# Gather holds, the place of the turns, and the opening products of a DLRM tower kernel on one core

## The reference

```python
e = jnp.stack([tbl_0[ids[:, 0]], ..., tbl_25[ids[:, 25]]], axis=1)      # (512, 26, 128)
combined = jnp.concatenate((dense_features[:, None, :], e), axis=1)      # (512, 27, 128)
interactions = jnp.einsum('bfd,bgd->bfg', combined, combined)
z = jnp.concatenate((dense_features, interactions[:, iu, ju]), axis=1)   # iu, ju: upper triangle
h = jnp.concatenate([z, dense_features], axis=1)                         # (512, 607)
h = jnp.maximum(h @ W_top1 + b_top1, 0.0)                                # 607 x 512
h = jnp.maximum(h @ W_top2 + b_top2, 0.0)                                # 512 x 256
y = h @ W_top3                                                           # 256 x 1
```

## Time and profile before

| | |
|---|---|
| median of the runs | 125.9 us (124.06 to 126.88) |
| the profiled execution | 124.81 us, span 123.0 us |
| TensorE matmuls busy | 104.2 us, 85% |
| VectorE, ScalarE busy | 65.4 us, 48.1 us |
| GpSimd busy | 65.7 us, of it 65.0 us in 60 gathers |
| chain that ended last | TensorE 83%, "issue" 13%, VectorE 2%, ScalarE 1% |

### The profile page before, as it was taken

One profiled execution on the slowest core, in us unless ns is written; L12 is line 12 of the kernel. 1 busy time (PEld: TensorE's weight loads), 2 busy tenths in 40 slices (PEclk: granted clock), 3 DMA queues, 4 the chain that ended last, 5 costly groups with the idle time before them and its releaser, 6 DMA issues.

```text
span 123.0 us, 3436 instructions
## 1 busy us (share of the span) xinstructions
PE 104.2 (85%) x1516; PEld 87.9 (71%) x1516; DVE 65.4 (53%) x110; ACT 48.1 (39%) x81; POOL 65.7 (53%) x66
## 2 busy tenths in 40 slices
PE   6999999999999999962178996289995299998993
PEld 6787888888888888831067895177992278996991
DVE  2599999999899996820001742105540106451411
ACT  4542979197794931300000462002541102730321
POOL 3887888579878887877500887503778305000000
PEclk9999999999999999999555999756999558999999
DMA  3799999999211112121200111200112100000000
GB/s 57 236 400 365 402 398 408 410 392 368 80 43 45 45 43 48 44 63 43 64 5 5 43 43 43 64 0 0 45 43 64 43 0 20 23 0 0 0 0 1
DMA packets 3949, 13.51 MB, mean 110 GB/s; under 512 B 1315, under 2 KB 1317, under 8 KB 3302
## 3 DMA queue, kind: packets, MB, share of 16 engines
q1 hardware_dynamic: 2018, 9.48, 20.5%
q0 software_dynamic: 1920, 3.94, 11.2%
q10 hardware_dynamic: 4, 0.00, 0.0%
HBM read 13.42 MB, written 0.00 MB: 109 GB/s over the span
## 4 chain that ended last, share of the span: by engine, by line
PE 83%; issue 13%; DVE 2%; ACT 1%
PE bank L365 17%; PE prod L408 13%; PE bank L414 13%; PE prod L365 12%; PE bank L374 7%; PE bank L504 6%; PE prod L433 4%; PE bank L321 4%; PE bank L325 3%; PE bank L445 2%; DVE inter_s L585 1%; PE bank L438 1%; PE prod L421 1%; PE bank L421 0%; DVE xT L575 0%
## 5 line engine op out<-in xcount | busy, mean ns | idle before, releaser
L313 POOL DMA_INDIRECT emb<-in_tbl,ids_sb x60 | 65.0, 1083 | 38.3 <-PE prod L408 19.3
L522 DVE TENSOR_SCALAR mask<-ids_h,ids_sb 128x1024 fp32r<-128x1024 int16 (+1 forms) x48 | 31.5, 699 | 2.2 <-issue 0.8
L408 PE MATMUL prod<-xT 128*27 128x27 f32 x1024 | 16.8, 215 | 14.7 <-issue 14.2
L408 PEld LDWEIGHTS prod<-xT 128*27 128x27 f32 x1024 | 13.6, 128 | 18.8 <-issue 17.4
L585 DVE STREAM_TRANSPOSE inter_s<-prod 128x288 f32<-128x288 f32 (+1 forms) x8 | 4.6, 611 | 26.3 <-PE prod L408 26.3
L365 PE MATMUL bank<-mask,high 128*128 128x512 f32 x46 | 15.2, 393 | 0.0
L365 PE MATMUL bank<-mask,low 128*128 128x512 f32 x46 | 15.0, 390 | 0.0
L414 PE MATMUL bank<-pairs,w_sb 117*128 117x128 f32 x96 | 12.7, 282 | 0.1
L414 PEld LDWEIGHTS bank<-pairs,w_sb 117*128 117x128 f32 x96 | 11.6, 191 | 0.7 <-ACT pairs L696 0.5
L531 DVE TENSOR_TENSOR low<-table,high 128x1024 fp32r<-128x1024 f32 (+1 forms) x9 | 11.7, 1301 | 0.0
L374 PE MATMUL bank<-ident,emb 128*128 128x128 f32 x60 | 10.5, 310 | 0.9 <-issue 0.9
(11 more groups left out here) (55 smaller groups left out, 118.1 us busy)
## 6 DMA issues: line engine op xcount, KB each, us to landing
table<-in_resident SPq DMA_DIRECT2D x3, 1024.0 KB
w_sb<-in_weights SPq DMA_DIRECT2D x1, 1792.0 KB
table<-in_resident SPq DMA_DIRECT2D x1, 1280.0 KB
table<-in_resident SPq DMA_DIRECT2D x4, 256.0 KB
emb<-in_tbl,ids_sb POOLq DMA_INDIRECT x60
ids_h<-in_other_ids SPq DMA_DIRECT2D x1, 896.0 KB
table<-in_resident SPq DMA_DIRECT2D x1, 640.0 KB
ids_h<-in_pair_ids SPq DMA_DIRECT2D x1, 256.0 KB
```

Of the source, the lines that this page charges most:

```text
L313: nc.gpsimd.indirect_dma_start(out=rows(t, c), out_offset=None, in_=gathered[c], in_offset=bass.IndirectOffsetOnAxis(ap=ids_sb[:, i:i + 1] ...
L408: mm = nc.tensor.matmul(prod[SLOT_PITCH * q:SLOT_PITCH * q + SLOTS, i, 0:SLOTS], x, x, start=True, stop=True)
L522: nc.vector.tensor_scalar(made(step)[:, 0:n, :], ids_h[:, 2 * b:2 * b + n, :], col_sb[:, row:row + 1], None, ALU.is_equal).then_inc(s_mask, 1)
```

## The change

Four edits. `hold` is gone, so GpSimd waits only where a gather would overwrite rows not yet turned. In passes 2 and 3 nothing stands between the two halves of the products: group 0 of the next tile is turned behind them, with group 1; only the first pass turns group 0 of tile 1 between the halves, with the dense part. `turn_next` gets a branch for that. Ahead of the lookups the products of ones are 3 and then 2 of 128 columns (before: 4 and 7 of 64 columns), and then 6 that are 32 wide in rows and columns.

```diff
-WARM_UP, WARM_KEEP = 4, 7
-WARM_COLUMNS = 64
+WARM_UP, WARM_KEEP, WARM_NARROW = 3, 2, 6
+NARROW = 32
...
-            def hold(t, i):
-
-
-                if (t, i) == (1, 0):
-                    pool.wait_ge(s_used, first_step[2])
-                if (t, i) == (1, 8):
-                    pool.wait_ge(s_used, first_step[3] + 2)
-                if (t, i) == (2, 0):
-                    pool.wait_ge(s_used, first_step[4] + 3)
-                if (t, i) == (2, 6):
-                    pool.wait_ge(s_used, first_step[5] + 3)
-                if (t, i) == (2, 10):
-                    pool.wait_ge(s_prod, 1)
-                if (t, i) == (3, 0):
-                    pool.wait_ge(s_l1, 2)
-                if (t, i) == (3, 4):
-                    pool.wait_ge(s_prod, 2)
-                if (t, i) == (3, 9):
-                    pool.wait_ge(s_l1, 4)
-                if (t, i) == (3, 13):
-                    pool.wait_ge(s_prod, 3)
...
                     for c in range(first, first + n):
-                        hold(t, c)
                         i = t * GATHERED + c
...
+            def turn_second(some):
+                for g in some:
+                    pe.wait_ge(s_gather[1][g], 16 * GROUPS[g][1])
+                    turn(1, g)
...
                     with nc.tensor.If(p < TILES):
                         for g in some:
-                            bank_free(g)
-
-                            pe.wait_ge(s_gather[1][g], (p + 1) * (8 * GROUPS[g][1]))
-                            turn(1, g)
+                            if g:
+                                bank_free(g)
+
+                                pe.wait_ge(s_gather[1][g], (p + 1) * (8 * GROUPS[g][1]))
+                                turn(1, g)
+                            else:
+                                with nc.tensor.If(p > 1):
+                                    pe.wait_ge(s_gather[1][g], 32 * GROUPS[g][1])
+                                    turn(1, g)
...
-            def keep_busy(n):
+            def keep_busy(n, rows=P):
                 for _ in range(n):
-                    nc.tensor.matmul(half_bank[1][:, 0:WARM_COLUMNS], warm, warm[:, 0:WARM_COLUMNS], start=True, stop=True)
+                    nc.tensor.matmul(half_bank[1][0:rows, 0:rows], warm[:, 0:rows], warm[:, 0:rows], start=True, stop=True)
...
             keep_busy(WARM_KEEP)
+            keep_busy(WARM_NARROW, NARROW)
             look_up_first()
...
                 products(range(MATMULS // 2))
-                turn_next(p, (0,))
                 with nc.tensor.If(p < 2):
+
+                    turn_second((0,))
                     dense_part(slice(0, P), (0, 1))
                 products(range(MATMULS // 2, MATMULS)).then_inc(s_prod, 1)
...
-                turn_next(p, (1,))
+                turn_next(p, (0, 1))
```

## The result

The changed kernel takes 137.0 us (median of 4 runs, 135.42 to 141.1) against 125.87 us (4 runs, 124.06 to 126.88). The ratio is 1.085, with a 95% interval of 1.062 to 1.108. The forecast was 131.0 us, with a range up to 133.5 us: the direction was right, the size too small by about half.

What follows compares the result with a forecast made beforehand. Behind the lookups GpSimd, too, was taken to bound the kernel, its gathers slowing TensorE's products. Later passes 1 and 2, less 6.4 us in pass 3, gave span 129.0 against 123.0, so 130.8, put at 131.0 us; range 123.5 to 133.5.

Steps and rivals of the forecast that it cites:

- The mechanism in the loop: Products: while gathers are issued, TensorE gets 2 to 4 records per us after 17 to 39 fast ones.
- the forecast case: Pass 1: both halves of the products crawl beside gathers; 131.0 us, own range 128.5 to 133.5, chance 0.52.
- The rival that the second half escapes: Pass 1: gathers slow its second half too late, products end at 72.2; 127.2 to 127.4 us, chance 0.20.
- the crawl of its own length: Products: a gather only sets the crawl off, it ends by itself after 5 to 8 us; 119.1 us, chance 0.14.
- the gathers that are not the cause: Products: the crawl belongs to the first half whatever GpSimd does; 124.7 us, chance 0.14.
- Lookup holds: Lookups: GpSimd waited once, 1.00 us where 0.30 is usual; without it gathers come 0.7 us earlier, bounds nothing to 1.0.
- the loop's 6 us: Four passes of the loop: later products in passes 1 and 2, 6.4 us back in pass 3; span 6.0 us more.
- The opening: Ahead of the lookups: first lookup near 5.7 instead of 7.39, 0.9 us gained, worth nothing in the forecast.
- upper and lower six: First lookup's products: six upper take 2.67 us, end near 8.4; six lower end near 10.65, against 11.54.
- The turns: Passes 3 and 4: the four turnings moved between the products add 0.4 us each time.

Runs made afterwards that it cites:

- n_gather: Kernel before without the 30 gathers of tiles 2 and 3, computed from rows of tiles 0 and 1; slow chip: 103.95 us against 126.22.
- b_none3: Kernel before with all of hold() and its call removed, old turns and opening; slow chip: 132.82 us against 125.3, ratio 1.068.
- sp_loads2: Kernel before without the 30 gathers of tiles 2 and 3, SyncE's queue loading 24 blocks of rows instead; quick chip: 104.3 us against 106.95.
- a_all: Changed kernel with the nine holds put back (new opening and new turns alone); slow chip: 123.98 us against 125.56, ratio 0.986.
- after3: The changed kernel run a third time, on a slow chip: 132.39, 141.44 and 145.89 us against 125.56 for the kernel before.
- a_oldopen: Changed kernel with the old products of ones (4 and 7 of 64 columns); slow chip: 132.73 us against 125.56, ratio 1.057.
- b_warm: Kernel before with the new products of ones alone; quick chip: 105.98 us against 106.58, ratio 0.996.
- b_turns: Kernel before with the new place of the turns alone, holds and opening as before; slow chip: 123.33 us against 126.22.
- before_again: The kernel before, unchanged, run again for its trace on a quick chip: 106.84 us.

## Why the prediction was right or wrong

*The mechanism in the loop was right, on the slow chips: gathers beside the products make TensorE crawl.* `n_gather` shows the cause (22 us go with the gathers), `b_none3` the steps. The forecast for the changed kernel against what `b_none3` measured: first half of pass 1 ends at 68.3, measured 69.0; gather 45 at 69.7, 70.71; second half ends at 76.9, 77.2; gather 49 at 78.3, 79.03; pass 2 fast again at 93.3, 94.8; pass 3 starts at 104.8, 106.3; span 129.0, 130.5. `b_none3` still turns group 0 between the halves, so it is a neighbour of the forecast case, not the same. In the changed kernel itself the steps of pass 1 could be seen only in part, since its first half ran free. The rival that the second half escapes fell (50 fast records, then a crawl to 76.3); so did the crawl of its own length and the gathers that are not the cause. The Trainium skill (SBUF — State Buffer, "SBUF: two separate sides") has the rule that a DMA and a compute operation can't slow each other. Read as the prediction read it, that gathers can't be what slows the products, it doesn't hold here: 126.22 us with the 30 gathers, 103.95 without, and the measurement decides. For the transfer alone the trace of `sp_loads2` agrees with it, on a quick chip (1.27 us a half). Which path gathers and engines share was not found.

*The step that failed is the term "Lookup holds".* It read one wait of 1.00 us, took from it that the gathers come 0.7 us earlier, and had no price for the lookups themselves. The argument beside it was that layers and turns run under gathers without idle time, which holds for the lookups of the kernel before, too. But the crawl isn't tied to products: the traces show it in VectorE's and ScalarE's masks, and once each in two traces GpSimd itself is late. The changed kernel's trace has its first product 24.0 us later, and 7.7 us given back in the loop, since by then most gathers were through. That sum, not the loop's 6 us, makes the long executions. What starts this crawl, and whether taking the lookup holds away is what lets it run on, stays open: `a_all` suggests the second, no experiment shows it.

How the measured 11 us divide is only roughly known. Without the holds and with clean lookups the ratio is 1.068 (`b_none3`); the change as a whole has 1.085, and the intervals overlap. The rest is probably the lookups' crawl. By its own sum the forecast should also have been 131.9 and not 131.0: 129.0 + 1.8 is the profiled execution, and the runs' median lies 1.1 us above that. The executions in which the lookups are clean (`b_none3`, 132.35) or may be (132.39 in `after3`; 131.68, 132.51 and 132.95 in `a_oldopen`) come close to it. All four of the first comparison, 135.42 and up, don't.

*The opening came out near the forecast, in part by luck.* First lookup at 5.7, measured 5.86; upper and lower six done at 10.65, measured 10.74, against 11.53. But two terms in between were off and made up for each other: the upper six took 3.31 us and not 2.67, since they waited for masks, and the lower six 1.57 and not 2.25. The wide products of ones took 0.275 us each (6 in 1.65), not 0.23; with that price the 12 narrow ones took (1.93 - 4 x 0.275) / 12 = 0.07, where 0.08 was taken. In other traces with the new opening the lower six took 1.36 to 2.46 us, and in two of them nothing was gained by their end: 11.51 in `a_all`, 12.03 in `b_warm`. The opening's 0.4% on a quick chip (`b_warm`, 0.992 to 1.000) can hardly be told from nothing, and on a slow one it was not measured alone.

*The turns were undervalued.* I had them at plus 0.4 us twice. With one branch between the halves and not three, the 256 records of a free pass take 2.56 us, against 3.09 before (110.08 to 113.17); and `b_turns` gained some 2% on a slow chip.

*The condition of the chip was not thought of at all.* The kernel before is 19 us slower on a slow chip than on a quick one, and the crawls were what I took for a property of the kernel. On a quick chip the sign is the other: 0.991.

For a slow chip the holds stay. With them, the new turns alone (`b_turns`) and the new turns with the new opening (`a_all`, three executions, 0.986, 0.972 to 0.999) both came out 1 to 2% faster, and the runs don't say which is the better. On a quick chip neither was run.

## What to carry to other kernels

Idle time named "issue", on several engines at once and only while GpSimd's indirect DMAs run, may be a cost of the gathers: take the gathers out once and see what goes. A wait that idles its own engine for 1 us may be what lets others recover, so its price is not read from its own idle time. And where a kernel stands idle without a releaser, run it on a second chip before tuning the schedule around it: here one and the same change is 1% faster or 8% slower.

## What the runs showed of the hardware

- The same program takes 106.6 to 107.0 us on two chips and 125.3 to 126.2 us on three; without 30 gathers it takes 104 us on a slow one. The two levels of the clock, the 0.94 us of a gather and the matmuls' own rates are the same; the mean granted clock is not, 0.90 to 0.93 on the slow chips and 0.98 to 1.00 on the quick ones and in `n_gather`.
- In the crawl TensorE's product records come in groups of 1 to 6, 0.7 us or twice that apart (80.66 to 85.56 in the changed kernel: 46 fast, then 22 in 4.9 us). Even on a quick chip gathers stretch 128 records from 1.27 to 1.81 us, at the full clock. That the gathers slow the supply of instructions is a reading that fits engines without a missing input; no row shows it. The packets that load instructions are not what is slowed, as far as the page tells: the larger of their two queues has 4 packets in the kernel before on a slow chip, with 0.2% of the time of the 16 DMA engines, and 4 with 0.3% in `before_again` on a quick one, so about 4 us (0.002 x 16 x 123.0) and 5 us (0.003 x 16 x 104.7) for the four.
- Loads of the same rows from SyncE's queue and memsets on GpSimd left the products at 1.27 us, the first on a quick, the second on a slow chip.
